# Key/value products between the score bursts, and values placed in three pieces: a two-layer transformer tower on one core

## The reference

```python
h = _L0_tok_ref(x, ...)                          # patch convolution + positions
h = _layernorm(h + _L0_attn_ref(h, ...))         # layer 0: attention over channels
h = _layernorm(h + _L0_ffn_ref(h, ...))          # 8 experts, top 2
h = _layernorm(h + _L1_attn_ref(h, ...))         # 12 heads, difference of two softmaxes
h = _layernorm(h + _L1_ffn_ref(h, ...))          # adapters + attention

# _L0_attn_ref, per image and head (8 heads of 24 channels, 2 query groups)
attn = jnp.einsum('bghnd,bghne->bghde', k, v)    # 24 x 24: keys times values, over tokens
attn = jax.nn.softmax(attn, axis=-1)
out  = jnp.einsum('bghde,bgne->bghnd', attn, qs)
out  = out.transpose(0, 2, 1, 3).reshape(b, n, c) @ Wproj + bproj
```

## Time and profile before

| | |
|---|---|
| median of 3 executions | 344.23 us (342.46 to 349.1) |
| profiled execution | 344.64 us, of which the span is 342.7 us |
| PE, PE weight loads | 87%, 74% of the span |
| DVE, ACT, POOL | 46%, 29%, 34% of the span |
| mean granted clock of PE | 0.924 of full |
| chain that ended last | PE 64%, DVE 11%, issue 11%, POOL 7%, DMA 4%, ACT 2% |

### The profile page before, as it was taken

How to read it: one execution, slowest core, us unless ns; L and a number is a source line. 1 busy time by engine, 2 the same in 40 slices (tenths; PEclk the granted TensorE clock), 3 DMA queues, 4 the chain that set the end, 5 groups by cost and what they waited for, 6 DMA issues and landing times.

```text
span 342.7 us, 7355 instructions
## 1 busy us (share of the span) xinstructions
PE 298.8 (87%) x3022; PEld 254.3 (74%) x3022; DVE 156.6 (46%) x463; ACT 97.9 (29%) x224; POOL 115.6 (34%) x177
## 2 busy tenths in 40 slices
PE   8966789998799999999999946986688979999991
PEld 8855678874599899999999825974466765748780
DVE  3752445759311311111111056457388647374665
ACT  4741114451011010111111103467233210483230
POOL 8370000183513474334431404536421310062402
PEclk9996765998989999999999995999699999999997
DMA  7999300020119678999994040000000000000002
GB/s 257 360 295 309 91 6 0 3 70 2 46 23 315 204 263 261 293 307 296 281 295 150 34 143 0 2 3 0 2 2 3 2 2 0 0 3 3 2 2 72
DMA packets 12036, 37.73 MB, mean 110 GB/s; under 512 B 1914, under 2 KB 5882, under 8 KB 11771
## 3 DMA queue, kind: packets, MB, share of 16 engines
q1 hardware_dynamic: 10083, 33.32, 30.5%
q0 software_dynamic: 1920, 3.93, 3.9%
HBM read 34.06 MB, written 3.19 MB: 109 GB/s over the span
## 4 chain that ended last, share of the span: by engine, by line
PE 64%; DVE 11%; issue 11%; POOL 7%; DMA 4%; ACT 2%; SPq 0%; POOLq 0%; DVEq 0%
PE ps L861 10%; PE ps L849 7%; PE ps L848 7%; PE ps L891 4%; PE ps L926 4%; PE ps L612 3%; PE ps L1040 3%; DMA xs<-x_rows,from_row 2%; PE ps L715 2%; POOL v_bd L573 2%; PE ps L912 2%; PE ps L731 1%; PE ps L937 1%; PE ps L692 1%; PE ps L636 1%
## 5 line engine op out<-in xcount | busy, mean ns | idle before, releaser
L849 PE MATMUL ps<-xgb,w1u 65*128 65x128 f32 x240 | 47.4, 279 | 0.0
L848 PE MATMUL ps<-xga,w1t 128*128 128x128 f32 x240 | 47.3, 279 | 0.0
L1620 DVE COPY ys<-ps 128x192 f32<-128x192 f32 x20 | 7.2, 358 | 79.8 <-PE ps L861 79.8
L1220 ACT ACTIVATE hid<-ps 128x768 f32<-128x768 f32 x20 | 16.2, 810 | 93.6 <-PE ps L849 93.6
L861 PE MATMUL ps<-w1t,hid 128*128 128x192 f32 x240 | 42.2, 326 | 0.0
L534 POOL DMA_INDIRECT y_rows<-ys,to_row x20 | 19.8, 988 | 59.5 <-DVE ys L1620 59.2
L861 PEld LDWEIGHTS ps<-w1t,hid 128*128 128x128 f32 x240 | 38.6, 190 | 0.0
L849 PEld LDWEIGHTS ps<-xgb,w1u 65*128 65x128 f32 x240 | 37.3, 195 | 0.0
L848 PEld LDWEIGHTS ps<-xga,w1t 128*128 128x128 f32 x240 | 37.1, 194 | 0.0
L501 POOL TENSOR_TENSOR rstd<-veps,neg_half 128x2 f32<-128x2 f32 (+1 forms) x16 | 10.6, 660 | 77.8 <-DVE veps L1508 77.8
L573 POOL COPY v_bd<-v_f 32x192 f32<-32x192 f32 x64 | 22.5, 351 | 38.0 <-ACT v_f L1110 34.3
(11 more groups left out here) (253 smaller groups left out, 585.5 us busy)
## 6 DMA issues: line engine op xcount, KB each, us to landing
w1t<-in_wt SPq DMA_DIRECT2D x20, 960.0 KB, 5.4
w1u<-in_wu SPq DMA_DIRECT2D x20, 240.0 KB, 7.6
pat<-in_pat SPq DMA_DIRECT2D x6, 496.0 KB, 6.4
w1a<-in_w1a SPq DMA_DIRECT2D x1, 1322.0 KB
y<-y_rows SPq DMA_DIRECT2D x6, 192.0 KB, 3.3
w1b<-in_w1b SPq DMA_DIRECT2D x1, 835.2 KB
x_rows<-x_tok SPq DMA_DIRECT2D x3, 192.0 KB, 2.0
out<-x_tok SPq DMA_DIRECT2D x6, 96.0 KB, 1.7
```

Of the source, the lines that this page charges most:

```text
L848: pe.matmul(out, w1t[:, b, 128 * k:128 * k + 128], xga[:, j % 2, :], start=True, stop=False)
L849: mm = pe.matmul(out, w1u[0:CB + 1, b, 128 * k:128 * k + 128], xgb[:, j % 2, :], start=False, stop=True)
L1220: act.activation(hid[:, j % 2, :], z, ACT.Relu).then_inc(hid_done, 1)
```

## The change

Nothing of the arithmetic changes, only which engine does a step and in which order.

- PE, first layer: the score bursts `keys_by_values` stand between the `keys_values` products instead of behind four of them; `queries(1)` moves behind `keys_by_values(5)`; `turn_a0(1)` and `by_queries` are spread; the four residual tiles stand ahead of `turn_a0(2)`; `keep_busy(5, 4)` is gone. In `keys_values` the product with `x0_lo` comes third instead of last.
- The low part `x0_lo` goes from POOL to DVE (`low0`), between DVE's own steps on x. ACT's `x0_out` is split, so that `tail_out(1)` comes ahead of the first tail.
- All eight `kv_out` are on ACT (DVE had four).
- The two multiplications of `norm0` go to POOL for rounds 0 to 2 (`weighted0`), and stay on DVE for round 3. `st0` has a fourth row for it.
- ACT: `exp0(0)` behind four `kv_out`, `exp0(1)` behind all, then `q0_out(1)`, `a0T_out(0)`, `exp0(2)`. DVE: `q0_out(1)` stands between `norm0(1)` and `shift0(2)`.
- POOL, layer 2: `place_values(0, 1)` comes in pieces of 4, 6 and 6 copies behind `add_sets(1)`, `(2)` and `(3)`, instead of all 16 behind `add_sets(0)`.

```diff
@@ -391,6 +392,12 @@
         O0_BANK = [6, 0]
+        def weighted0(r, gg):
+
+            inv = st0[:, 2 + r % 2, :].rearrange("p (i g a) -> p g i a", i=IG, g=2)[:, gg]
+            return (a0[:, r % 2, gg, :, :, 0:D0], e0[:, r % 2].rearrange("p (i g a) e -> p g i a e", i=IG, g=2)[:, gg],
+                    bass.AP(tensor=inv.tensor, offset=inv.offset, ap=[list(d) for d in inv.ap] + [[0, D0]]))
+
         block = ctx.enter_context(nc.Block())
@@ -486,13 +493,19 @@
                 pool.wait_ge(x0_done, 2 * n + 2)
                 pool.wait_ge(x0_high, 2 * n + 2)
-                pool.tensor_tensor(slotted(x0_tail[CB:128], n), dense_half(xpb[0:CB], n), slotted(x0_tail[0:CB], n).bitcast(F32), ALU.subtract).then_inc(x0_low, 1)
-                pool.wait_ge(x0_low, 2 * n + 1)
-                pool.tensor_tensor(slotted(x0_lo, n), dense_half(xpa, n), slotted(x0_hi, n).bitcast(F32), ALU.subtract).then_inc(x0_low, 1)
-                pool.wait_ge(x0_low, 2 * n + 2)
+                pool.tensor_tensor(slotted(x0_tail[CB:128], n), dense_half(xpb[0:CB], n), slotted(x0_tail[0:CB], n).bitcast(F32), ALU.subtract).then_inc(x0_tails, 1)
+                pool.wait_ge(x0_tails, n + 1)
             low_first(0)
             low_first(1)
+            for r in range(3):
+                pool.wait_ge(inv_ready, r + 1)
+                wait(pool, a0T_ready, r - 1)
+                for gg in range(2):
+                    out, part, inv = weighted0(r, gg)
+                    ins = pool.tensor_tensor(out, part, inv, ALU.mult)
+                ins.then_inc(a0_ready, 1)
+                pool.wait_ge(a0_ready, r + 1)
             def rsqrt(layer):
                 for pair in range(PAIRS):
@@ -560,18 +573,18 @@
                 pool.wait_ge(x_cast, 3 * n + 2)
                 pool.tensor_tensor(tokens(xt_lo[0:CB], n), images(xpb[0:CB], n), tokens(xt_hi[0:CB], n).bitcast(F32), ALU.subtract).then_inc(x_split, 1)
-            def place_values(call, n):
+            def place_values(call, n, first, last):
                 pool.wait_ge(v_flat, 4 * call + 2 * n + 2)
                 if call:
                     pool.wait_ge(o1_ready, G)
                 pool.wait_ge(x_split, 2 * n + 2)
-                for i in range(IG):
-                    for h in range(HQ):
-                        src = view(v_f[32 * i:32 * i + 32, 4 * n, 16 * h:16 * h + 1], [[C, 4], [64, 3], [1, 16]])
-                        dst = view(v_bd[32 * h:32 * h + 32, 4 * n * IG + i, 0, 16 * h:16 * h + 1], [[IG * C, 4], [64, 3], [1, 16]])
-                        pool.tensor_copy(dst, src).then_inc(v_placed, 1)
-                        pool.wait_ge(v_placed, 32 * call + 16 * n + HQ * i + h + 1)
+                for k in range(first, last):
+                    i, h = k // HQ, k % HQ
+                    src = view(v_f[32 * i:32 * i + 32, 4 * n, 16 * h:16 * h + 1], [[C, 4], [64, 3], [1, 16]])
+                    dst = view(v_bd[32 * h:32 * h + 32, 4 * n * IG + i, 0, 16 * h:16 * h + 1], [[IG * C, 4], [64, 3], [1, 16]])
+                    pool.tensor_copy(dst, src).then_inc(v_placed, 1)
+                    pool.wait_ge(v_placed, 32 * call + 16 * n + k + 1)
             def add_sets(g):
@@ -583,15 +596,23 @@
                 pool.tensor_tensor(p1[:, g % 2, 2, :, 0:N], blk[:, 0, 2], blk[:, 1, 2], ALU.add).then_inc(p1_ready, 1)
             low_parts(0)
-            place_values(0, 0)
+            place_values(0, 0, 0, 16)
             low_parts(1)
             add_sets(0)
-            place_values(0, 1)
-            for g in range(1, G):
+            add_sets(1)
+            pool.wait_ge(p1_ready, 2)
+            place_values(0, 1, 0, 4)
+            add_sets(2)
+            pool.wait_ge(p1_ready, 3)
+            place_values(0, 1, 4, 10)
+            add_sets(3)
+            pool.wait_ge(p1_ready, 4)
+            place_values(0, 1, 10, 16)
+            for g in range(4, G):
                 add_sets(g)
             rsqrt(2)
-            place_values(1, 0)
-            place_values(1, 1)
+            place_values(1, 0, 0, 16)
+            place_values(1, 1, 0, 16)
             rsqrt(3)
         PREP = 14
@@ -671,18 +692,20 @@
                 if g % 4 == 0:
                     pe.wait_ge(x0_high, g // 2 + 2)
                 if g >= 2:
-                    pe.wait_ge([kv_act, kv_dve][g % 2], g // 2)
+                    pe.wait_ge(kv_act, g - 1)
                 pe.matmul(out, padded(x0_hi, g), wkv_hi[:, 0, :], start=True, stop=False)
                 pe.matmul(out, padded(x0_hi, g), wkv_lo[:, 0, :], start=False, stop=False)
                 if g % 4 == 0:
-                    pe.wait_ge(x0_low, g // 2 + 2)
+                    pe.wait_ge(x0_low, g // 4 + 1)
+                pe.matmul(out, padded(x0_lo, g), wkv_hi[:, 0, :], start=False, stop=False)
+                if g % 4 == 0:
+                    pe.wait_ge(x0_tails, g // 4 + 1)
                 pe.matmul(out, padded(x0_tail, g), wkv_hi[:, 1, :], start=False, stop=False)
-                pe.matmul(out, padded(x0_tail, g), wkv_lo[:, 1, :], start=False, stop=False)
-                pe.matmul(out, padded(x0_lo, g), wkv_hi[:, 0, :], start=False, stop=True).then_inc(kv_ready, 1)
+                pe.matmul(out, padded(x0_tail, g), wkv_lo[:, 1, :], start=False, stop=True).then_inc(kv_ready, 1)
             def keys_by_values(g):
-                pe.wait_ge([kv_act, kv_dve][g % 2], g // 2 + 1)
+                pe.wait_ge(kv_act, g + 1)
                 if g and g % 2 == 0:
                     pe.wait_ge(s0_shifted, g // 2)
                 for a in range(2):
...
@@ -735,32 +761,33 @@
             pe.wait_ge(w0_in, 32)
             pe.wait_ge(pool_set, PREP)
             queries(0)
-            for g in range(4):
-                keys_values(g)
+            keys_values(0)
+            keys_values(1)
             keys_by_values(0)
+            keys_values(2)
             keys_by_values(1)
-            queries(1)
+            keys_values(3)
             keys_values(4)
+            keys_by_values(2)
             keys_values(5)
-            keys_by_values(2)
             keys_by_values(3)
             keys_values(6)
             keys_values(7)
             keys_by_values(4)
             keys_by_values(5)
+            queries(1)
             pe.wait_ge(const_in, 16)
             turn_a0(0)
-            turn_a0(1)
-            by_queries(0)
-            by_queries(1)
             keys_by_values(6)
             keys_by_values(7)
-            turn_a0(2)
+            by_queries(0)
+            turn_a0(1)
+            by_queries(1)
             pe.wait_ge(s0_shifted, 4)
             for t in range(4):
                 residual(t)
+            turn_a0(2)
             by_queries(2)
-            keep_busy(5, 4)
             turn_a0(3)
             by_queries(3)
             pe.wait_ge(a0T_done, 4)
...
@@ -1174,19 +1204,21 @@
             act.wait_ge(pool_set, PREP)
             tail_out(0)
-            x0_out(0)
+            x0_heads(0)
             tail_out(1)
-            x0_out(1)
+            x0_ends(0)
+            x0_heads(1)
+            x0_ends(1)
             q0_out(0)
-            kv_out(0)
-            kv_out(2)
+            for g in range(4):
+                kv_out(g)
             exp0(0)
+            for g in range(4, G):
+                kv_out(g)
+            exp0(1)
             q0_out(1)
-            kv_out(4)
-            exp0(1)
-            kv_out(6)
+            a0T_out(0)
             exp0(2)
-            a0T_out(0)
             a0T_out(1)
             exp0(3)
             a0T_out(2)
@@ -1397,6 +1429,12 @@
                     for s, m in ((0, CA), (1, CB)):
                         dve.tensor_scalar(pos[0:m, s, :], pos_t[0:m, s, 0:N], pos_t[0:m, s, N:N + 1], None, ALU.add).then_inc(pos_ready, 1)
+            def low0(n):
+
+                dve.wait_ge(x0_done, 2 * n + 1)
+                dve.wait_ge(x0_high, 2 * n + 1)
+                dve.tensor_tensor(slotted(x0_lo, n), dense_half(xpa, n), slotted(x0_hi, n).bitcast(F32), ALU.subtract).then_inc(x0_low, 1)
+
             def x0_out(n):
                 tok = slice(HALF * n, HALF * n + HALF)
@@ -1404,20 +1442,19 @@
                 again = lambda m, s: view(pos[0:m, s, 0:1], [[0, B // 2], [1, N]])
                 dve.wait_ge(conv_done, n + 1)
                 dve.tensor_tensor(dense0(xpa[:, tok]), dense0(ps[:, n, 0:HALF]), again(CA, 0), ALU.add).then_inc(x0_done, 1)
+                if n:
+                    low0(0)
                 dve.wait_ge(tail_copied, n + 1)
                 dve.tensor_tensor(dense0(xpb[0:CB, tok]), dense0(xpb[0:CB, tok]), again(CB, 1), ALU.add).then_inc(tail_summed, 1)
                 dve.wait_ge(tail_summed, n + 1)
                 dve.tensor_tensor(xpb[0:CB, tok], xpb[0:CB, tok], ps[0:CB, 2 + n, 0:HALF], ALU.add).then_inc(x0_done, 1)
+                if n:
+                    low0(1)
             dve.wait_ge(pos_ready, 2)
             dve.wait_ge(pool_set, PREP)
             x0_out(0)
             x0_out(1)
-
-            def kv_out(g):
-
```

(43 more changed lines are left out.)

1 line of the change is left out of this document (added).

## The result

The changed kernel takes **348.13 us** (median, 346.83 to 348.39, 4 runs) against 345.1 (342.46 to 349.1, 4 runs) for the one before beside it: ratio 1.0136, 95% interval 1.0087 to 1.0185. It is 1.4% slower, with the interval clear of 1, where I forecast 340 and at most 346.5. The profiled execution took 348.06 us, span 346.2 (342.7 before), mean granted clock 0.912. Some executions of every kernel here take over 1.5% longer than its fastest: ratios leave them out, medians and ranges do not.

The account below looks back on a forecast made before the run. PE bounds the kernel (64%), short of instructions in the first layer and waiting for POOL in layer 2. The profiled 344.64 plus 0.7 lost in the first layer minus 5.3 gained in layer 2 gives 340; range 332 to 346.5.

Parts of the forecast that it names:

- Layer 2: Values placed in pieces let `add_sets(1)` start at 237.4, `scores(0, 4)` 4.9 us earlier; gain 5.3, bounds 4.3 and 6.
- Low part and blocks: First layer: `x0_lo` on DVE saves 1.0 us; stops at 256-instruction blocks stay, resuming at 28.1, 37.0 and 42.1.
- The wait for `q0_out(1)` and `shift0(2)`: First layer: new 1.9 us wait of `keys_by_values(6)` for DVE's subtraction, covering `turn_a0(0)`.
- At most 7.3 us after, where no stop shows: Instruction fetch after the third stop: the block, asked for on entering the one before, takes at most 7.3 us.
- Turn and eviction at half clock: First layer's tail: `turn_a0` 0.6 us at half clock (0.5 at full), its eviction 0.6.
- all-half sum: Steps up to `by_queries(3)` all at half clock: it starts at 61.6; with only the queries at full clock, 60.3.
- 0.8, bounds 0 and 3.4: Behind `by_queries(3)`, without `keep_busy`: loss from more half clock there and in the projections, 0.8 us taken.
- The Trainium skill's rule against idle gaps: Idle time between matmul bursts brings the lower clock back; by it alone the sum with everything at half clock, 61.6.
- Rival 3: First layer: block asked for at 22.5 takes 8.8 us, not 5.65, resumptions 3.1 later; total 347, chance 0.1.
- companion, half clock: Part of the slower case: PE idles more, all runs at half clock, 1.3 us more, projections 2.6 more.
- the filler's removal: First layer without the four `keep_busy`: a further stretch at half clock likely behind `by_queries(3)`, 0.8 us.

Follow-up runs that it names:

- experiment 1: Kernel before the change with only layer 2's values placed in three pieces: 338.85 us, ratio 0.9802.
- experiment 10: Changed kernel with bursts and `queries(1)` in the order of before, the new tail kept: 343.77 us, ratio 1.007.
- Experiment 11: Changed kernel with PE's whole order of before, but without the filler `keep_busy(5, 4)`: 333.71 us, ratio 0.975.
- experiment 9: Changed kernel with PE's order of before from `turn_a0(0)` on (the tail), bursts in their new order: 334.97 us, ratio 0.9792.
- experiment 5: Changed kernel with `turn_a0(2)` ahead of the four residual tiles and the filler `keep_busy(5, 4)` put back: 340.71 us, ratio 0.9984.
- 2: Changed kernel with layer 2's values placed as before, 16 copies behind the first addition: 354.71 us, ratio 1.0337.
- 4: Changed kernel with DVE doing `shift0(2)` ahead of `q0_out(1)`: 345.29 us, no usable ratio.
- 8: Changed kernel with PE's whole order of before, `keep_busy` included: 334.38 us, ratio 0.9696.
- experiment 12: Changed kernel with PE's order of before, late weights loaded first and experts' weights held back until layer 1's scores are done: 326.32 us, ratio 0.9533.
- experiment 6: Kernel before with values in three pieces, experts' and late weights issued only after layer 1's last score product: 335.85 us, ratio 0.9814.

## Why the prediction was wrong

- **Layer 2, right.** Gain 5.3 forecast, 5.6 in the trace, 4.6 in experiment 1's medians.
- **Low part and blocks, right.** Stops by 256 records at 27.00, 35.58 and 40.88 (forecast 28.1, 37.0, 42.1). They came 1.1 to 1.4 us earlier than forecast: PE entered the first block at 22.71, about as forecast, but that fetch and its crossing took 4.3 us, not 5.65.
- **The wait for `q0_out(1)` and `shift0(2)`, right**: 1.67 us at 44.88, after `turn_a0(0)`.
- **Where the 8 us went.** By the profiled executions, 348.06 against 340.0 forecast: the way to `by_queries(3)` took 2.5 more (62.80 for 60.3), from there to the statistics the loss was 3.2 for 0.8, another 3.36 came behind them where I had put nothing, and layer 2 gave 0.34 more than forecast. That makes 7.9.
- **"At most 7.3 us after, where no stop shows": the step that failed first.** I took a block to be asked for when PE enters the one before. Asking in fact waited for PE to pass its wait for the subtraction, which I had forecast myself. The landing 2.05 us after that wait and 1.36 to resume give the stop of 2.34, which was missing from the sum.
- **Turn and eviction at half clock, mis-sized.** Each pair took 1.74 or 1.75 us (50.57 to 52.31, 57.48 to 59.23, 61.06 to 62.80), where I had 0.6 + 0.6. From `turn_a0(2)` to `by_queries(3)` it was 62.80 - 57.48 = 5.32, not 0.6 + 4.05, and not by ACT's 2.79: `o0_out(0)` ended at 61.99 and PE waited 0.69. PE's own two turns and one product, with both evictions uncovered, set it.
- **The sum redone.** My all-half sum was 61.6. The earlier start (-1.2), the rest of the scores (-0.1), `queries(1)` at full clock (1.45 for 2.7), DVE's wait (2.27 for 1.9), the stop (2.34), `turn_a0(1)` with its eviction (0.54 more), the last piece (0.67 more) and smaller differences give 62.8, which is what was measured.
- **"0.8, bounds 0 and 3.4" for the clock behind it: it cost as much.** The first statistics came 5.62 late, 2.42 by `by_queries(3)` and 3.2 in the projections, which I had bounded rightly but chosen at the wrong end. Another 3.36 came between 70 and 233 us, where I had only a shift. 1.92 of it is the half clock to 227.4 over layer 2's first products. The other 1.44 lie between the statistics and these products: 153.08 us in the changed kernel, 151.64 before, 151.67 in experiment 10, and 150.09 in experiment 1, so single profiles differ by that much there. Why the clock differed is not settled. The Trainium skill's rule against idle gaps (TensorE: Matmul & The Clock Gate), which I weighed and set aside for the middle, pointed the right way: from 46.5 us on all was at half clock. The idle gaps that the rule speaks of are longer than the 0.69 us here, though, so this trace does not test it.
- **Rival 3** had the sign and nearly the time (347) with the wrong place: the first fetch was no slower, the fourth was asked for late. Its companion, half clock, was right from 46.5 us on.
- **I blamed the filler's removal.** Experiment 11 shows that it costs nothing with the order of before; in the new order that is open. The full clock stayed away where the tail was cut up: `by_queries(0)`, `(1)` no longer ahead of the last bursts, and waits of 0.69 us for evictions between turn and product, three times. With all of the old tail it was back at 47.5 (experiment 9), with `turn_a0(2)` ahead of the tiles and the filler at 58.7 (experiment 5), in one profile each.

Shown: the halves add up (1, 2); the block's request follows the wait (4); the tail costs the time (8 to 10). The order of `turn_a0(2)` and the tiles, with the filler, is worth 7 of it (5, ratio 0.9984 for 1.0136). Argued only: how the tail's 9 to 13 us divide between stop and clock. By the traces of the two pairs that differ in the tail alone, it is 6.7 and 7.0 us at `by_queries(3)` (62.80 for 56.06, 61.74 for 54.73) and 3.2 more at the statistics in both.

## What to carry to other kernels

Work that is free of the next wait belongs ahead of it, in one piece: spreading independent bursts as cover for single waits left PE three uncovered evictions, one late block and a half clock that reached into the projections. Before moving a wait in a stream of many small instructions, count records to the next 256 and see where PE will stand when it has to ask. And keep bulk loads that nobody needs yet out of such a stretch: that was worth about 8 us here (334.38 to 326.32), once the weights needed first were loaded first.

## What the runs showed of the hardware

- **When a block is asked for.** The packet of the next 256 instructions started 1.10 us after a wait of PE early in the current block had ended (44.74 to 45.84, 43.10 to 44.20), up to 5 us after the crossing, took 0.95 us without other traffic, and PE went on 1.36 us after it. Beside the weight loads (share 0.93) from crossing to landing took 7.3 us (27.00 to 34.30), without them and without such a wait about 2.2 (31.0 to 33.25 in experiment 12). The Trainium skill (Runtime: NRT & Kernel Launch, Instruction fetch mechanics) has the next block fetched while the current one executes. The trace agrees that the packets start ahead of PE's last instructions (32.97 and 38.28 in the changed kernel, PE out of work at 33.8 and 40.1). That this hides the fetch held in experiment 6, where no burst stops; beside weight loads or behind a wait PE stood still for 0.8 to 2.3 us in the changed kernel.
- **The half clock lasts over broken work.** In the changed kernel PE was busy 20.19 of 23.90 us at 1.2 GHz with waits of 0.69 us in between. It came back to 2.4 GHz while it worked without gaps: at 70.4 in work that began at 62.80, at 58.7 in work from 53.5 in experiment 5, at 47.5 in work from 40.9 in experiment 9.
